# A small MLP joined to the clustered attention ahead of it, on one core

## What is computed

```python
def _reference_tuple_inner(inputs, ln1_g, ln1_b, Wq, ..., W1, b1, W2, b2):
    x = _layernorm(inputs, ln1_g, ln1_b)
    attn_out, extra_loss = _lha_attention(x, Wq, Wk, Wv, Whq, Whk, Wo)
    x = attn_out + inputs
    y = _layernorm(x, ln2_g, ln2_b)
    y = jax.nn.relu(jnp.einsum('bsd,dm->bsm', y, W1) + b1)
    y = jnp.einsum('bsm,md->bsd', y, W2) + b2
    return (x + y, extra_loss)
```

## Time and profile before

| | us |
|---|---|
| time, median of 3 runs | 1464.22 (1463.91 to 1464.61) |
| profiled execution | 1465.65 |
| its span in the trace | 1463.8 |

### The profile page before, as it was taken

The page is one execution under the profiler, slowest core; times in us unless marked ns, Lnnn a source line. Parts: engine busy times, 40 slices in busy tenths (PEclk is TensorE's granted clock), DMA queues, the critical chain, the costliest instruction groups (busy, mean ns, idle before and its releaser), DMA issues.

```text
span 1463.8 us, 27861 instructions
## 1 busy us (share of the span) xinstructions
PE 1268.3 (87%) x9636; PEld 643.2 (44%) x9636; DVE 1090.7 (75%) x1943; ACT 998.3 (68%) x2313; POOL 822.2 (56%) x1005
## 2 busy tenths in 40 slices
PE   3378989998998988679589999998988999999898
PEld 1112222222222322157256666665534666666554
DVE  4778888888888877223489999995447999999644
ACT  4236766676666666577488999985337999999632
POOL 3666666667766640022577888870028888877200
PEclk9659999999999999989799999999999999999999
DMA  3523333343334330010111111110101111111001
GB/s 103 110 42 65 73 59 65 60 79 58 66 58 73 65 59 1 1 57 1 37 26 27 27 30 27 28 27 2 47 15 42 31 30 27 27 27 31 1 17 41
DMA packets 161120, 60.87 MB, mean 42 GB/s; under 512 B 139691, under 2 KB 152789, under 8 KB 160981
## 3 DMA queue, kind: packets, MB, share of 16 engines
q1 hardware_dynamic: 160980, 59.09, 19.1%
HBM read 8.60 MB, written 2.10 MB: 7 GB/s over the span
## 4 chain that ended last, share of the span: by engine, by line
PE 29%; ACT 11%; DVE 7%; issue 4%; POOL 2%; ACTq 0%; DVEq 0%; POOLq 0%
ACT la_s L1735 8%; PE la_ring L1360 6%; PE la_ring L1372 3%; PE la_s L1393 3%; PE la_pT L1467 3%; DVE la_prob L1624 2%; PE la_pT L1406 2%; PE la_m L1539 2%; PE la_ring L1455 1%; PE la_pT L1457 1%; PE la_s L1455 1%; PE la_s L1457 1%; ACT la_v_own L1777 1%; PE la_s L1385 1%; PE la_o L1422 1%
## 5 line engine op out<-in xcount | busy, mean ns | idle before, releaser
L618 DVE TENSOR_REDUCE row_max<-max_ps 128x2 f32<-128x1024 f32 x256 | 312.9, 1222 | 70.6 <-PE max_ps L430 69.2
L670 ACT ACTIVATE prob<-scores_ps 128x1024 f32<-128x1024 f32 x256 | 262.2, 1024 | 147.8 <-PE scores_ps L410 144.3
L1735 ACT ACTIVATE la_s<-la_s,la_bias,la_inv 128x128 f32<-128x128 f32 x512 | 223.4, 442 | 7.0 <-DVE la_bias L1612 7.0
L1886 POOL TENSOR_TENSOR la_turned<-la_raw,lw_rot 128x1024 f32<-128x1024 f32 x64 | 150.9, 2358 | 115.6 <-PE la_ring L1372 70.1
L1360 PE MATMUL la_ring<-lw_wqkv,la_hT 128*128 128x512 f32 x384 | 202.4, 638 | 15.3 <-DVE la_swapped L1587 6.7
L410 PE MATMUL scores_ps<-stack 128*128 128x512 f16 x512 | 155.7, 386 | 42.0 <-ACT prob L670 41.1
L1892 POOL TENSOR_TENSOR la_turned<-la_turned,la_swapped 128x1024 f32<-128x1024 f32 x64 | 150.7, 2355 | 5.0
L444 PE MATMUL heads_ps<-prob,v_pad 128*32 128x512 f32 x1024 | 137.2, 608 | 1.1 <-ACT prob L670 1.1
L430 PE MATMUL max_ps<-stack 24*128 24x512 f16 x512 | 102.5, 397 | 31.2 <-DVE row_max L618 18.5
L410 PEld LDWEIGHTS scores_ps<-stack 128*128 128x128 f16 x512 | 34.2, 97 | 208.7 <-ACT prob L670 161.3
L1587 DVE TENSOR_TENSOR la_swapped<-la_ring,lw_rot 128x256 f32<-128x256 f32 x256 | 90.8, 415 | 33.3 <-ACT la_raw L1746 23.8
(11 more groups left out here) (177 smaller groups left out, 2765.7 us busy)
## 6 DMA issues: line engine op xcount, KB each, us to landing
la_v_back<-la_v_own SPq DMA_DIRECT2D x112, 128.0 KB, 2.3
X<-in_x SPq DMA_DIRECT2D x8, 256.0 KB, 5.4
stack<-stack_tok SPq DMA_TRANSPOSE x128, 3.2
out<-X SPq DMA_DIRECT2D x8, 256.0 KB, 2.3
lw_wqkv<-in_wqkv SPq DMA_DIRECT2D x2, 768.0 KB, 4.8
stack<-shift_row SPq DMA_DIRECT2D x64, 2.0 KB
lw_rot<-in_rot SPq DMA_DIRECT2D x2, 512.0 KB, 6.5
lw_w<-in_fw SPq DMA_DIRECT2D x2, 341.0 KB
```

Source lines behind the costliest of these rows:

```text
L618: nc.vector.tensor_reduce(row_max[:, grp % 2, w // 2, :, w % 2], max_ps[:], AX.X, ALU.max).then_inc(max_made, 1)
L670: nc.scalar.activation(prob[:, c % 4, 2 * pr:2 * pr + 2, :], scores_ps[:], ACT.Exp, scale=1.0 / LOGIT_SCALE).then_inc(exp_made, 1)
L1735: ins = nc.scalar.activation(s_ps[:, place(h), :], s_ps[:, place(h), :], ACT.Exp, bias=bias[:, T % 2, h:h + 1], scale=inv[:, T % 4, h:h + ...
L1886: nc.gpsimd.tensor_tensor(spun, raw[:, T % 2].rearrange("p s (h f) -> p s h f", f=LD), rot[:, T % TPB, :, 0, :].unsqueeze(2).to_broadcast( ...
```

## The change

The function `mlp_and_turn` is gone, and its steps stand in the lists of `clustered_attention`. The slots go on past the attention's end; from slot 239 (`MLP_SLOT`) on, seven slots make one round of the MLP, and each step has its place in the round (`mlp_at` gives round m and place k). So rounds -1, 0 and the first slots of 1 and 2 run beside the last 17 Exps and the last output of attention. There is one barrier less. The other parts:

- Memory: y, yT, hid, base and w lie in the half of `stack` that even batches use, v_pad lies in XT. In PSUM the first product uses the banks of the maxima (and from batch 3 on those of the scores too), the second product, the turned input and output use bench banks and `heads_ps`. From slot 236 on the bench has two banks.
- The input's moments are no longer made for all batches at once. For each batch VectorE aggregates them in slot 32b+41, GpSimd adds epsilon and takes the power -0.5 in slot 32b+42, VectorE makes the shift in slot 32b+43. The same on GpSimd takes the place of square root and reciprocal for the output. ScalarE needs no table of square roots there.
- The weights of the local layers' first products (wqkv, gains, rot) are loaded at the start of the kernel; the tables, wo and the ffn weights at the start of the local layers, with semaphores of their own.

```diff
-LAST_SLOT = B * SLOTS + 10
+LAST_SLOT = B * SLOTS + 16
+MLP_SLOT = B * SLOTS - 17
+MLP_STEPS = 7
...
+        def mlp_at(n):
+            return (n - MLP_SLOT) // MLP_STEPS - 1, (n - MLP_SLOT) % MLP_STEPS
+        def run(slot):
+            for n in range(FIRST_SLOT, MLP_SLOT + MLP_STEPS * (B + 4)):
+                slot(n)
+        def h_bank(b, c):
+            return max_ps[:, c % 2, :] if b < 3 or c < 2 else scores_ps[:, c % 2, :]
+        def o_bank(b):
+            return bench_ps[:, 2, :] if b < 2 else bench_ps[:, 0, :] if b % 2 == 0 else heads_ps[:]
...
         @block.tensor
+            def turn_input(b):
+                pe.wait_ge(y_made, b + 1)
...
+                elif b in (3, 4):
+                    pe.wait_ge(added, b - 2)
...
+            def mlp_slot(n):
+                m, k = mlp_at(n)
+                if k == 0 and batch_or_none(m + 1) is not None:
+                    turn_input(m + 1)
+                if k == 0 and batch_or_none(m - 3) is not None:
+                    turn_output(m - 3)
+                if 1 <= k <= MC and batch_or_none(m) is not None:
+                    first_product(m, k - 1)
+                if k > MC and batch_or_none(m - 1) is not None:
+                    second_product(m - 1, k - MC - 1)
...
         @block.vector
-                    nc.vector.bn_stats(stats[:, t, :], Z[:, t, :])
+                    nc.vector.bn_stats(stats[:, t, :], Z[:, t, :]).then_inc(tok_stats_done, 1)
+                dve.wait_ge(tok_stats_done, (x + 1) * TPB)
+                for t in range(x * TPB, (x + 1) * TPB):
+                    nc.vector.bn_aggr(in_moments[:, t, :], stats[:, t, :]).then_inc(in_moments_done, 1)
+            def input_shift(b):
+                at = slice(b * TPB, (b + 1) * TPB)
+                dve.wait_ge(in_inv_done, b + 1)
+                nc.vector.scalar_tensor_tensor(out=in_shift[:, at], in0=in_moments[:, at, 0], scalar=-1.0,
+                                               in1=in_inv[:, at], op0=ALU.mult, op1=ALU.mult
+                                               ).then_inc(in_shift_done, 1)
...
+            def mlp_slot(n):
+                m, k = mlp_at(n)
+                b = every(n - SLOTS - 11, SLOTS, B)
+                if b is not None:
+                    input_shift(b)
+                if k == 1 and batch_or_none(m - 2) is not None:
+                    output_shift(m - 2)
+                if k == MLP_STEPS - 1 and batch_or_none(m - 1) is not None:
+                    add_second(m - 1)
...
         @block.scalar
+                if k == 1 and batch_or_none(m + 1) is not None:
+                    take_yT(m + 1)
+                if 2 <= k < 2 + MC and batch_or_none(m) is not None:
+                    hidden(m, k - 2)
+                if k == MC and batch_or_none(m - 3) is not None:
+                    take_turned(m - 3)
+                if k == MLP_STEPS - 1 and batch_or_none(m + 2) is not None:
+                    centre(m + 2)
+                if k == MLP_STEPS - 1 and batch_or_none(m - 2) is not None:
+                    normalise(m - 2)
...
         @block.gpsimd
+            def invert_input(b):
+                at = slice(b * TPB, (b + 1) * TPB)
+                pool.wait_ge(in_moments_done, (b + 1) * TPB)
+                nc.gpsimd.tensor_tensor(in_var[:, at], in_moments[:, at, 1], mlp_eps[:, 0], ALU.add
+                                        ).then_inc(in_var_done, 1)
+                pool.wait_ge(in_var_done, b + 1)
+                nc.gpsimd.tensor_tensor(in_inv[:, at], in_var[:, at], power[:], ALU.pow).then_inc(in_inv_done, 1)
...
+                b = every(n - SLOTS - 10, SLOTS, B)
+                if b is not None:
+                    invert_input(b)
+                if k == 2 and batch_or_none(m - 1) is not None:
+                    add_base(m - 1)
+                if k == MLP_STEPS - 1 and batch_or_none(m - 1) is not None:
+                    invert_output(m - 1)
...
         @block.sync
             for dst, src in loads:
                 sp.dma_start(dst, src).then_inc(w_loaded, 16)
+            for dst, src in early_loads:
+                sp.dma_start(dst, src).then_inc(early_loaded, 16)
```

More of the change, by code:

```diff
@@ L507, in _, with both @@
+            def both(n):
+                if n < LAST_SLOT:
+                    slot(n)
+                mlp_slot(n)
+            run(both)
         @block.vector
```

489 lines of the change are left out of this document (229 added, 260 removed).

## The result

The changed kernel took **1476.47 us** (median of five runs, 1472.64 to 1480.71) against 1464.61 for the kernel before beside it: a ratio of 1.0079, 95% interval 1.0063 to 1.0095. It is slower by 0.8%, as forecast (1475.0, range 1464 to 1484). Its runs scatter over 8 us, those of the kernel before over 3. The profiled execution is the fastest of the five, with a span of 1470.9 us against 1463.8, so it is 7.1 longer. A median run has 4 us more. Falls of TensorE's clock, of which the experiments give the price, are the likely reason; no trace of a median run shows it.

The account below looks back on a forecast made before the run. TensorE was taken to bound the running MLP, an Exp-scores loop attention's last slots, and VectorE-TensorE maxima its body. Seam -11.8, stalls +18.6, clock +3.9, start +0.3 gave +11.0 us: 1475 us, range 1464 to 1484.

Parts of the forecast that it names:

- The wait on VectorE: Attention's body: VectorE's shift waits for GpSimd's late power, delaying TensorE's maxima; six stalls of 3.1 us, 18.6 us lost.
- the bound of 16: Lower end for the six stalls in attention's body, 2.7 us each: 16 us lost.
- The case in which the scaling also comes first: Attention's body: VectorE's shift also waits for GpSimd's scaling behind the copy; the 18.6 us loss grows up to 22.5.
- The clock: Attention's stalls: TensorE's clock falls in three of six, 1.3 us each, 3.9 us lost.
- The seam: Clustered attention to small MLP, slot 238's Exp to last copy into XT: 108.2 us against 120.0, gain 11.8.
- the prediction's last part: Signs for right or wrong, among them TensorE's clock staying at 1.00 at the seam.
- The start: Kernel start: three early loads may share DMA engines with the start's loads; 0.3 us lost, 0 to 1.
- are not the same: Sign against the prediction: local layers, from the last copy into XT on, differing from 761.6 us.
- 1: Attention's stalls: the clock does not fall; +7.1 us, 1471.3 us; chance 0.27.
- 2: Attention's stalls: the clock falls each time and stays low for two slots; +23 us, 1487 us; chance 0.07.
- 3: Attention's body: VectorE's stall is made up; 1452.7 us, chance 0.08 in full or most; halfway near 1464, 0.08.
- 4: Seam: TensorE not filled because ScalarE's centrings are late; gain 3 us instead of 12, 1484 us; chance 0.08.

Follow-up runs that it names:

- e1: The changed kernel with VectorE's input shift of each batch four slots later; 1457.86 us, ratio 0.9954 to the kernel before.
- e6: The changed kernel with VectorE's input shift of each batch one slot later; 1461.48 us, ratio 0.9977 to the kernel before.
- e3: The changed kernel with the three early loads (wqkv, gains, rot) issued at slot 32; 1481.89 us, ratio 1.0107 to the kernel before.
- e4: The changed kernel with GpSimd's add_base moved ahead of invert_output in its queue; 1474.94 us, ratio 1.0072 to the kernel before.
- e7: The changed kernel with GpSimd's addition and power ahead of the query share of their slot; 1461.26 us, ratio 0.9969 to the kernel before.

## Why the prediction was right, point by point

**The wait on VectorE: mechanism right, size 3.1 forecast and 2.5 found.** The steps up to the end of row_max were right to 0.3 us: TensorE's maxima came at 194.67, and by the prediction's working, moved by the 1.9 us by which this batch is late, they come at 195.0. The power took 1.04, as in the earlier trace rows. Two steps of the size failed. The maxima were taken as 3.1 us late and are 2.6 to 2.9 late in the six batches, measured against e1. And what TensorE's maxima lose was taken for what the batch loses: another 0.3 comes back some 12 us later (e6). So six stalls cost 15.1 us instead of 18.6; the bound of 16 was too high. The shift was taken at 0.42 and took 0.23: it ended with GpSimd's copy (192.87 and 192.88), with nothing on top. Alone, in e1, it took 0.15. The Trainium skill (SBUF — State Buffer, Who interferes with whom) has the one that starts first take the port for the whole of its instruction. By that the shift, 0.07 behind the copy, lasts at least until the copy's end, and the trace agrees, here and in the tail, where it ends with GpSimd's base (702.21 + 1.27 and 702.26 + 1.23). The case in which the scaling also comes first, and the loss grows to 22.5, did not come about.

**The clock: right in number, low in price.** Three of six was taken; nine of eighteen fell in three kernels, one in the changed kernel, five in e3 and three in e4. So three is the mean, and no single trace but e4's had it. Taken at 1.3 us each; it was 1.5 for a short fall and 2.9 for a long one, so 5.4 a kernel instead of 3.9. The row that the price was taken from the earlier trace rows shows one Exp behind a slow pair of scores, and a long fall lasts over three slots. That an idle of 2.95 us was enough was a fair sign, and no more than an even one. The runs of the changed kernel without a trace point the same way, though not in strict order: the fastest, with one fall in its stalls, had a mean clock of 0.967, the slowest (1480.71) one of 0.959, the three between 0.963, 0.964 and 0.961. Stalls and falls together are 20.5 (15.1 and 5.4, the mean of the three kernels), 18.3 by the medians of the changed kernel and e1 through their ratios, and 22.5 was forecast. In the profiled execution itself they are 16.5, since only one fell.

**The seam: -9.5 against -11.8.** The 30.8 us that the prediction starts from go to the start of the last Exp (582.17 to 612.98). By these bounds slots 238 to 255 were taken at 36.5 and took 36.4 where the clock held; the rest was taken at 71.7 and took 72.6. In it are the late base as forecast (2.1 against 1.5) and rounds of 8.13 (7.88 and 0.25; 0.3 was forecast); the last product ended 63.4 us behind the start of the last Exp (62.2 forecast), and the chain behind it took 9.2 (9.5). The prediction's own terms add up to less than it used: 3.2 and not 3.5 for the new waits, 9.0 and not 9.5 for the chain. The other 1.6 is the fall of the clock in those slots, 38.0 instead of 36.4. That contradicts the prediction's last part, which had the clock at 1.00 there. It fell in all six traces with the base behind, and in one of four with it ahead. Whether the base has to do with that, when its operations stand on another engine, is open.

**The start: +1.2 in this trace, 0.3 forecast.** ScalarE went on from b_rows at 19.24, against 17.92 in the earlier trace rows, which is a little more than the bound of 1. e3 and e4 show it to be scatter for the most part.

**The local layers: 761.6 forecast, 758.9 found.** Nothing in them changed. The first products behind the MLP, before and then after:

```profile
711.76 2.08 PE L1360 MATMUL la_ring<-lw_wqkv,la_hT 128*128 128x512 f32 x2 [1.48 <-DVE la_swapped L1587]
...
714.52 3.78 PE L1360 MATMUL la_ring<-lw_wqkv,la_hT 128*128 128x512 f32 x4 [0.69 <-ACT la_v_own L1777]
```

```profile
721.52 1.12 PE L1405 MATMUL la_ring<-lw_wqkv,la_hT 128*128 128x512 f32 x2 [1.48 <-DVE la_swapped L1636]
...
723.34 1.98 PE L1405 MATMUL la_ring<-lw_wqkv,la_hT 128*128 128x512 f32 x4 [0.69 <-ACT la_v_own L1826]
```

0.96 + 1.80 = 2.76: in one the clock came back ahead of these six chunks, in the other behind them. From the last copy to the end it was 758.9 to 763.9 in the ten traces of the changed kernel and the experiments, whose local layers are the same program. Most of this scatter goes with the clock: in these stretches it was at its lower level for 21.6 us in the changed kernel (758.9), 23.3 in e1 (760.1), 29.5 in e7 (762.8) and 36.9 in e4 (763.9), and over the ten traces time and length have a correlation of 0.91. In the kernel before it was 31.2 us (761.6). So "are not the same" was a bad sign against the prediction: equal programs differ by 5 us here.

**The rivals.** The clock did fall (against 1), not each time (2), the wait was not made up (3, e6: 0.6 us of it at most), and TensorE was filled (4). Errors went both ways: stalls 3.5 too dear, falls 1.5 too cheap, seam 2.3 too good. So 1475.0 against 1476.5 is nearer than its terms are, and that much is luck. The rest was taken at nothing, and the traces bear it out. The moved aggregations and the values in XT: the batches of e1 are those of the kernel before. The tables and weights at the head of the local layers: from the last copy to the first product there it is 4.31 us in both traces (702.22 to 706.53, 711.98 to 716.29), and behind it no engine's idle time ends with a DMA in either trace.

## What to carry to other kernels

Before a step is put into a pipelined order on two engines, look where the *producer's* queue stands when the consumer gets there, not at which slot both are written: here the price was one slot's worth of GpSimd's other work, and moving the consumer four slots or the producer one step made it vanish. Here an idle of 2.6 us on TensorE cost about itself plus an even chance of a clock fall (nine of eighteen), and with one of 3.6 us the clock fell all six times. When a change has a good part and a bad one, find the bad one by its own idle line first: the seam's 9.5 us were there from the start, hidden under 20.
